# Two attention layers and two expert layers: the dispatch fill in parts, four row buffers, and a last expert that leaves by tiles

## The reference, cut to what matters

```python
x = x + L0_xattn(layernorm(x), ctx)      # quantised self- and cross-attention, softmax, projection
x = x + L0_ffn(layernorm(x))             # 8 experts, top 2, capacity 640, relu
x = x + L1_xattn(layernorm(x), positions, tokens)   # grouped attention, rms norm, rope
x = x + L1_ffn(layernorm(x))             # 8 experts, top 2, no capacity, silu(gate) * up
```

```python
h = relu(dispatched @ w1); out[token] += gate * (h @ w2)              # L0_ffn
y = (silu(x @ w_gate) * (x @ w_up)) @ w2; out[token] += gate * y      # L1_ffn
```

## Time and profile before

| | us |
|---|---|
| median of 3 runs | 3048.16 |
| lowest, highest | 3046.93, 3048.58 |
| profiled execution, its time | 3051.39 |
| its span, first to last instruction | 3049.6 |
| first attention, experts | 0 to about 1140, about 1140 to 2020 |
| second attention, experts | 2021 to 2757, 2760 to 3049.6 |

### The profile page before, as it was taken

How to read it: one execution, slowest core, us unless ns; L and a number is a source line. 1 busy time by engine, 2 the same in 40 slices (tenths; PEclk the granted TensorE clock), 3 DMA queues, 4 the chain that set the end, 5 groups by cost and what they waited for, 6 DMA issues and landing times. The chain is left out here.

```text
span 3049.6 us, 57678 instructions
## 1 busy us (share of the span) xinstructions
PE 2834.9 (93%) x16353; PEld 1636.1 (54%) x16354; DVE 1807.4 (59%) x5590; ACT 1703.4 (56%) x4562; POOL 1749.1 (57%) x2443
## 2 busy tenths in 40 slices
PE   4699999999999969999999999959999999985998
PEld 2366666666666644555555555424555555543664
DVE  4366666666666646433443444539989988863443
ACT  5578777787777742332332333427777777751332
POOL 6467777777777624544453544447677777731222
PEclk9899999999999989999999999979999999998999
DMA  7711121111211145544554454735665555557444
GB/s 244 257 43 50 56 80 59 49 49 56 80 59 49 46 142 166 158 136 138 161 154 135 139 159 136 215 76 114 122 137 132 118 131 129 127 108 292 83 81 68
DMA packets 467530, 360.90 MB, mean 118 GB/s; under 512 B 295521, under 2 KB 366305, under 8 KB 467425
## 3 DMA queue, kind: packets, MB, share of 16 engines
q1 hardware_dynamic: 404912, 282.85, 32.5%
q0 software_dynamic: 16496, 37.79, 6.2%
q10 hardware_dynamic: 46016, 38.99, 4.4%
HBM read 186.23 MB, written 110.39 MB: 97 GB/s over the span
## 5 line engine op out<-in xcount | busy, mean ns | idle before, releaser
L1393 POOL TENSOR_TENSOR e_st<-e_st,e_ws_tile 128x1024 f32<-128x1024 f32 x64 | 123.9, 1936 | 429.0 <-PE e_y L1149 417.3
L752 ACT ACTIVATE a_nrm<-a_mm,a_sc_t 128x128 f32<-128x128 f32 x768 | 290.9, 475 | 123.5 <-POOL a_sc_t L905 123.3
L603 DVE BATCH_NORM_STATS2 a_st<-a_mm 128x6 f32<-128x128 f32 x768 | 170.5, 284 | 290.5 <-PE a_mm L440 208.0
L439 PE MATMUL a_mm<-a_w_hi,a_xq_hi 128*128 128x512 f16 x768 | 296.9, 387 | 23.3 <-POOL a_xq_lo L887 15.1
L1187 ACT ACTIVATE e_hh<-e_ha 128x512 f16<-128x512 f32 x128 | 76.3, 596 | 413.3 <-PE e_ha L1134 412.0
L440 PE MATMUL a_mm<-a_w_hi,a_xq_lo 128*128 128x512 f16 x768 | 297.0, 387 | 0.0
L1282 DVE SCALAR_TENSOR_TENSOR e_hl<-e_ha,e_hh 128x512 f16<-128x512 f32 x128 | 88.4, 691 | 351.7 <-ACT e_hh L1187 351.3
L904 POOL TENSOR_TENSOR a_sc_t<-a_sc_t,a_mhalf 128x4 f32<-128x4 f32 x192 | 204.1, 1063 | 118.5 <-DVE a_sc_t L610 118.2
L1148 PE MATMUL e_y<-e_w2l,e_hh 128*128 128x512 f16 x640 | 242.6, 379 | 0.0
L1147 PE MATMUL e_y<-e_w2h,e_hh 128*128 128x512 f16 x640 | 242.6, 379 | 0.0
L1149 PE MATMUL e_y<-e_w2h,e_hl 128*128 128x512 f16 x640 | 242.6, 379 | 0.0
(11 more groups left out here) (366 smaller groups left out, 8221.4 us busy)
## 6 DMA issues: line engine op xcount, KB each, us to landing
e_st<-in_w SPq DMA_DIRECT2D x128, 512.0 KB, 4.1
disp<-a_empty SPq DMA_DIRECT2D x16, 2084.0 KB, 8.0
e_st<-in_w1b SPq DMA_DIRECT2D x32, 352.0 KB, 3.1
disp<-a_empty SPq DMA_DIRECT2D x4, 2605.0 KB, 21.5
e_xb<-disp SPq DMA_DIRECT2D x40, 260.5 KB, 4.3
e_xb<-disp ACTq DMA_DIRECT2D x40, 260.5 KB, 2.7
a_cx<-in_ctxT SPq DMA_DIRECT2D x32, 256.0 KB, 3.3
a_stage<-in_wprojT SPq DMA_DIRECT2D x16, 512.0 KB, 4.9
```

Source lines behind the costliest of these rows:

```text
L439: pe.matmul(out, xq_hi[:, n, c, :], w_hi[:, t, c, :], start=(c == 0), stop=False)
L752: ins = act.activation(nrm[:, n % 2, i * P:(i + 1) * P], src[:, i * P:(i + 1) * P], ACT.Identity, bias=sc_t[:, n % 2, 3, i:i + 1], scale=s ...
```

## The change

1. The fill of `disp` leaves SP in eight DMAs of 5 tiles, in the even slots of batch 1, after the other steps of the slot; `r_scatter` waits for eight.
2. In the last expert of the first experts PE signals each tile of Y; DVE takes tiles 0, 2, 4 and ACT 1, 3, each signals by itself, and POOL adds each tile when it is out. The row numbers are copied without a wait.
3. The second experts have four buffers for rows; four loads go ahead of the loop, then tile i+3 in `x_high(i)`. The loop body holds four tiles on PE, ACT and DVE. One more tile of rows is loaded at the end (41 for 40).
4. In `add_rows` of the second experts the row numbers are copied before the wait for the add before.

```diff
-                    for n in range(4):
-                        sp.dma_start(disp[n * TILES // 4 * P:(n + 1) * TILES // 4 * P, :].rearrange("(c p) d -> p c d", p=P),
-                                     empty[:].unsqueeze(1).to_broadcast([P, TILES // 4, RW])).then_inc(sem["disp_filled"], 16)
+            def fill_disp(b, t):
+                if isinstance(b, int) and b == 1 and t % 2 == 0:
+                    lo, hi = (n * TILES // (NJ // 2) for n in (t // 2, t // 2 + 1))
+                    sp.dma_start(disp[lo * P:hi * P, :].rearrange("(c p) d -> p c d", p=P),
+                                 empty[:].unsqueeze(1).to_broadcast([P, hi - lo, RW])).then_inc(sem["disp_filled"], 16)
...
+            run_pipeline(sp, [("job", 0, lambda b, t: weights(b, t + 1)), ("att", 5, residual), ("end", 10, store), ("in", 1, x_load),
+                              ("job", 0, fill_disp)], NJ, SCORE_AT, head=HEAD)
...
-                pool.wait_ge(sem["disp_filled"], 16 * 4)
+                pool.wait_ge(sem["disp_filled"], 16 * (NJ // 2))
...
+                    if last and c == FC - 1:
+                        mm.then_inc(y_each, 1)
+                if not (last and c == FC - 1):
+                    mm.then_inc(y_done, 1)
...
+                for i in range(1, TPE, 2) if last else range(3, TPE):
+                    if last:
+                        act.wait_ge(y_each, i + 1)
                     ins = act.activation(yb[:, i, :], Y[i][:], ACT.Copy, scale=g_now[:, i:i + 1])
+                    if last:
+                        ins.then_inc(y_out[i % 2], 1)
...
+                for i in range(0, TPE, 2) if last else range(3):
+                    if last:
+                        dve.wait_ge(y_each, i + 1)
                     ins = dve.tensor_scalar(yb[:, i, :], Y[i][:], g_now[:, i:i + 1], None, ALU.mult)
+                    if last:
+                        ins.then_inc(y_out[i % 2], 1)
...
+            def add_rows(e, last=False):
+                if not last:
+                    pool.wait_ge(ya_ok, e + 2)
+                    pool.wait_ge(yv_ok, e + 2)
                 ch.link(pool.tensor_copy(r_now[:], row[:, bass.ds(e * TPE, TPE)]))
                 for i in range(TPE):
+                    if last:
+                        pool.wait_ge(y_out[i % 2], i // 2 + 1)
...
-        xb = s.sb("xb", [P, 2, RW], F32)
+        xb = s.sb("xb", [P, XBUF, RW], F32)
...
-            whole = (most_tiles - most) // 2
+            whole = (most_tiles - most) // XBUF
             with eng.Fori(0, whole) as n:
-                for q in range(2):
+                for q in range(XBUF):
                     for ahead, f in stages:
-                        f(2 * n + q + ahead, (q + ahead) % 2)
+                        do(f, XBUF * n + q + ahead, (q + ahead) % XBUF)
...
-                if not (isinstance(i, int) and i == 0):
+                if not (isinstance(i, int) and (i == 0 or i + XBUF - 1 > last_load)):
                     act.wait_ge(meta, i + 2)
-                    load(i + 1, 1 - q)
+                    load(i + XBUF - 1, (q + XBUF - 1) % XBUF)
...
-            load(0, 0)
-            load(1, 1)
+            last_load = XBUF * ((most_tiles - 2) // XBUF) + XBUF
+            for i in range(XBUF):
+                load(i, i)
...
             def add_rows(i, q):
                 pool.wait_ge(r_ok, i + 1)
                 pool.wait_ge(yev, i + 3)
+                ch.link(pool.tensor_copy(r_now[:, q:q + 1], row[:, bass.ds(i, 1)]))
                 if not (isinstance(i, int) and i == 0):
                     pool.wait_ge(added, 16 * i)
-                ch.link(pool.tensor_copy(r_now[:, q:q + 1], row[:, bass.ds(i, 1)]))
                 pool.sem_inc(y_free, 1)
```

More of the change, by code:

```diff
@@ L956 @@
 KEYS = 2 * P
+XBUF = 4
 W_NAMES = ["K", "Q0", "Q1", "Q2", "Q3", "V"]
@@ L1135, in hidden, with second @@
                     mm.then_inc(done, 1)
-            def second(e, c):
+            def second(e, c, last):
                 m = c // 2
@@ L1156, in body @@
                         hidden(e, c + 1, last)
-                    second(e, c)
+                    second(e, c, last)
                     if c in TILE_AT and not last:
@@ L1244, in body @@
                     columns(e + 1)
-                act.wait_ge(y_done, e * FC + FC + 2)
+                if not last:
+                    act.wait_ge(y_done, e * FC + FC + 2)
                 act.wait_ge(y_free, e + 1)
                 act.wait_ge(g_ok, e + 1)
-                for i in range(3, TPE):
+                for i in range(1, TPE, 2) if last else range(3, TPE):
+                    if last:
+                        act.wait_ge(y_each, i + 1)
                     ins = act.activation(yb[:, i, :], Y[i][:], ACT.Copy, scale=g_now[:, i:i + 1])
-                ins.then_inc(ya_ok, 1)
+                    if last:
+                        ins.then_inc(y_out[i % 2], 1)
+                if not last:
+                    ins.then_inc(ya_ok, 1)
             for j in range(TPE):
@@ L1365, in body @@
                     columns(e + 1)
-                dve.wait_ge(y_done, e * FC + FC + 2)
+                if not last:
+                    dve.wait_ge(y_done, e * FC + FC + 2)
                 dve.wait_ge(y_free, e + 1)
-                for i in range(3):
+                for i in range(0, TPE, 2) if last else range(3):
+                    if last:
+                        dve.wait_ge(y_each, i + 1)
                     ins = dve.tensor_scalar(yb[:, i, :], Y[i][:], g_now[:, i:i + 1], None, ALU.mult)
-                ins.then_inc(yv_ok, 1)
+                    if last:
+                        ins.then_inc(y_out[i % 2], 1)
+                if not last:
+                    ins.then_inc(yv_ok, 1)
                 ch.clear()
@@ L2062, in layer1_experts, with pipeline, do @@
         w_in = [s.sem(f"w_in{e}") for e in range(E)]
-        x_in = [s.sem(f"x_in{n}") for n in range(2)]
+        x_in = [s.sem(f"x_in{n}") for n in range(XBUF)]
         block = s.block()
-        def pipeline(eng, stages):
+        def pipeline(eng, stages, by_buffer=()):
             most = max(n for n, _ in stages)
+            def do(f, i, q):
+                f(i, q) if f in by_buffer else f(i, q % 2)
             for i in range(-most, 0):
@@ L2071, in pipeline @@
                     if i + ahead >= 0:
-                        f(i + ahead, (i + ahead) % 2)
-            whole = (most_tiles - most) // 2
+                        do(f, i + ahead, (i + ahead) % XBUF)
+            whole = (most_tiles - most) // XBUF
             with eng.Fori(0, whole) as n:
-                for q in range(2):
+                for q in range(XBUF):
                     for ahead, f in stages:
-                        f(2 * n + q + ahead, (q + ahead) % 2)
-            for i in range(2 * whole, most_tiles):
+                        do(f, XBUF * n + q + ahead, (q + ahead) % XBUF)
+            for i in range(XBUF * whole, most_tiles):
                 for ahead, f in stages:
                     if i + ahead < most_tiles:
-                        f(i + ahead, (i + ahead) % 2)
+                        do(f, i + ahead, (i + ahead) % XBUF)
         def first_two(i):
@@ L2182, in y_evict @@
                 act.activation(yb[:, q, :], YB[q][:], ACT.Copy, scale=1.0 / (WS * WS)).then_inc(yev, 1)
-            load(0, 0)
-            load(1, 1)
-            pipeline(act, [(2, x_high), (0, a_high), (1, silu_gate), (0, y_evict)])
-            act.wait_ge(x_in[most_tiles % 2], 16 * (most_tiles // 2 + 1))
+            last_load = XBUF * ((most_tiles - 2) // XBUF) + XBUF
+            for i in range(XBUF):
+                load(i, i)
+            pipeline(act, [(2, x_high), (0, a_high), (1, silu_gate), (0, y_evict)], (x_high,))
+            for n in range(XBUF):
+                act.wait_ge(x_in[n], 16 * ((last_load - n) // XBUF + 1))
         @block.vector
```

28 lines of the change are left out of this document (12 added, 16 removed).

## The result

The changed kernel takes 3019.7 us (median; 3017.5 to 3020.9), the one before 3047.55 in the same measurement: a ratio of 0.9903, 95% interval 0.9889 to 0.9917, so 27.9 us less. The forecast was 3011; the time lies inside the range, 9 us above its point. Ratios and their intervals in this document leave out one execution of part 2 alone that took 9036.8 us.

A forecast was written before the change was run, and what follows sets the result against it. TensorE (PE), busy 93% of the span, was taken as the bound, with waits at block starts, the joint and the end. Savings 21.5 + 4.7 + 9 + 1.8 = 37.0 off 3048.2 gave 3011 us, range 3005 to 3024.

The forecast's parts named there:

- the steady batch: First attention: distance of 63.6 us between later `cx_lo` marks on POOL, forecast to return once the stall goes.
- 85.1 us: First attention: first distance between `cx_lo` marks, 21.5 longer than the steady 63.6; the basis of part 1's -21.5.
- the joint: Between first experts and second attention: evictions by tile let POOL's adds issue earlier, taken -4.7 us.
- Counted from add 0's issue at 2787: Second experts: evictions waiting for adds to free output buffers give back 0.5 to 3 us of part 3's gain.
- 42.4 - 32.1 us: Second experts, transpose 2 to 7: 42.4 us for five tiles that take 32.1 at 6.41 each; 10.3 to gain.
- The 1.37 us of transpose 2: Second experts: transpose 2's own wait, added to the 10.3 to make part 3's 11.7 in all.
- the first term: First attention: with the fill spread, the stall for the load of `xt` goes, taken -21.5 us (-19.8 to -21.7).
- Rival A: Second experts: adds take the place of the loads, gain there 3 us or less, kernel at 3017; chance 0.15.
- Rival C: Second experts: doubled loop body makes PE stand for code at each of nine passes, kernel at 3056; chance 0.02.

The follow-up runs named there:

- part 2 alone: The kernel before with only the by-tile evictions in the last of the first experts: 3044.6 us, 0.9991 of the kernel before.
- four fills behind: The kernel before with its four large fill DMAs moved as they are behind the load of xt: 3027.0 us, 0.9933 of the kernel before.
- eight ahead: The changed kernel with all eight fill parts issued at once ahead of the load of xt: 3037.3 us, 0.9965 of the kernel before.
- parts 3 and 4 together: The kernel before with four row buffers and the row-number copy before the wait, nothing else: 3043.8 against 3046.8 us, 0.9988.

## Experiments: what held the second experts

**Four output buffers** (the changed kernel; an eviction waits for the add four tiles back rather than two).
```diff
-        yb = s.sb("yb", [P, 2, DM], F32)
+        yb = s.sb("yb", [P, 4, DM], F32)
...
-            act.sem_inc(y_free, 1)
+            act.sem_inc(y_free, 3)
```


> The changed kernel with four output buffers in place of two in the second experts: y_evict(i) waits for add i-4 instead of add i-2. Theory (the adds, 10 us each while the weights come in, are what holds the tiles once the row waits are gone): the adds stay as slow as they are, but ACT's waits for POOL (14.9 us in three) go, PE's transpose of tile 11 comes about 76 us after the block's start instead of 83.9, and the kernel gains 6 to 8 us on the changed one, 3011 to 3014. Rival (rows, weights and adds share so much that PE then waits for rows or weights instead): tile 11 stays at 82 or later, 3018 to 3020.

> The changed kernel with four output buffers once more, beside the two that build on it. It was 3014.1 us, 0.9888 of the kernel before. Expected 3013 to 3016 and a ratio of 0.988 to 0.990, from the add chain's release of the evictions; 3019 or more would mean that the first measurement was an outlier and that the buffers give nothing.


Measured: 3014.1 (0.9888 [0.9872, 0.9903]) and in a second measurement 3015.9 (0.9902 [0.9886, 0.9919]), against 3019.7 (0.9903 [0.9889, 0.9917]) for the changed kernel. Neither interval excludes no gain over it, and as a difference from the kernel before in the same measurement (-32.8, -30.0 against -27.9) the two are 5 and 2 us. The traces are clearer. In the first of them the evictions wait for PE in 38 tiles and none waits for a buffer, and PE's wait for `e_al` is down from 4.3 to 1.4 us:

```profile
ACT e_yb L2208 <- PE e_y L2175: 56.9, 38, 2.9
```
```profile
PE e_y L2173 <- DVE e_al L2264: 1.4, 1, 1.4
```

while the adds still leave 9.6 and 10.4 us apart:

```profile
2760.47 1.64 POOL L2285 DMA_INDIRECT out<-e_yb,e_r_now  x1 [0.84 <-POOL e_r_now L2281]
2770.08 1.59 POOL L2285 DMA_INDIRECT out<-e_yb,e_r_now  x1 [4.06 <-DMA out<-e_yb,e_r_now]
2780.51 1.57 POOL L2285 DMA_INDIRECT out<-e_yb,e_r_now  x1 [8.17 <-DMA out<-e_yb,e_r_now]
```

All kernels, grouped by their second experts (one profiled execution each; the two with paced weights are left out):

| kernels | tile 2 to tile 11, us | first load to end, us |
|---|---|---|
| rows two buffers: before, part 1, part 2, part 4, four fills behind | 67.1 to 68.1 | 288.2 to 290.0, mean 289.0 |
| part 3 without part 4 | 66.2 | 289.3 |
| parts 3 and 4: changed, eight ahead, parts 3 and 4 | 65.2 to 65.6 | 283.7 to 286.8, mean 285.4 |
| parts 3 and 4 and four output buffers: both measurements, and with the dummies below | 59.7 to 59.9 | 280.1 to 281.4, mean 280.5 |

So parts 3 and 4 are worth 3.6 us with two output buffers and 8.5 with four, and the 4.9 between them are what the adds took back. Four output buffers without parts 3 and 4 were not run. But in none of the five traces of the first row does an eviction wait for a buffer, so there they would have had no wait to take away.

**Weights paced** (the changed kernel; SP loads the weights of experts 3 to 7 only as tiles get done).
```diff
+                if e >= 3:
+                    sp.wait_ge(w_in[e - 1], 64)
+                    sp.sem_inc(w_ok, 1)
+                    sp.wait_ge(yd, 2 * (e - 2) + 2)
...
-                if e >= 1:
+                if 1 <= e < 3:
```


> The changed kernel with SP loading the weights of experts 3 to 7 of the last block only as tiles are done (expert e after 2(e-2) tiles), two output buffers as before. Theory (adds are slow because the weights fill the DMA engines): an add goes from about 10 us to 5 or 6, the tiles run every 6.4 us from the second on, tile 11 at about 76 to 78 us, 3012 to 3015. Rival (adds are slow by themselves at first, or because of the row loads ahead): adds still 9 to 10 us apart, 3018 to 3020.


Measured: 3021.3, 0.9913 [0.9899, 0.9927]: no gain. The early stretch is repaired (tile 2 to tile 11 in 59.6 us, add 1 is issued 6.4 us after add 0), but then ACT waits 21.6 us for buffers, 20.0 of them after the transpose of tile 11, and the later adds come 8 to 10 us apart where a paced expert's weights are loaded (POOL):

```profile
2761.26 1.64 POOL L2289 DMA_INDIRECT out<-e_yb,e_r_now  x1 [0.84 <-POOL e_r_now L2285]
2767.67 1.59 POOL L2289 DMA_INDIRECT out<-e_yb,e_r_now  x1 [0.86 <-POOL e_r_now L2285]
...
2804.93 1.57 POOL L2289 DMA_INDIRECT out<-e_yb,e_r_now  x1 [4.64 <-ACT e_yb L2212]
2814.64 1.57 POOL L2289 DMA_INDIRECT out<-e_yb,e_r_now  x1 [7.93 <-remote]
```

SP issues the weights of experts 4 to 7 at 2778.6, 2791.5, 2804.2 and 2819.1. Between adds that leave 8.1 to 10.3 us apart the core's DMA engines move 217 to 324 GB/s, between those 5.6 to 6.0 apart 88 to 164, and of the two steps of 6.4 us one has 111 and one 239. An add is slow when weights are in flight, whenever that is. This ties the 10 us to the weights' traffic and not to the start of the block. Nor are the deeper row loads the cause: in the kernel before, with two row buffers, the first adds leave 10.7, 9.1 and 9.5 apart.

**Four output buffers and paced weights.** The edits are the two above.


> The changed kernel with four output buffers and with the weights of experts 3 to 7 loaded one expert per two tiles done (as a_pace, 3021.3 us). Theory (the adds are slowed by whatever else fills the DMA engines): pacing only moves the weights' traffic to later tiles; the chain of adds is early faster and later slower, and at the end it stands where it stood in a_yb4, some 3 us behind PE: 3014, within 1.5 us of a_yb4. Rival (only the burst hurts): with slack of four buffers the chain makes up its lag, the last eviction lies 12.7 us before the end instead of 15.8: 3011.


Measured: 3014.9, 0.9893 [0.9877, 0.9910], within 1.0 us of both measurements of four buffers without pacing. In the profiled execution (3022.0, the longest of its four) the adds run one behind another to the end, mostly 6.4 us apart and the last five steps 5.5, and the last eviction lies 20.7 us before the end, 8 more than in the changed kernel: the chain did not make up its lag, rather the reverse. No gain of pacing is seen.

**Work for PE ahead of the first weights** (four output buffers, and 28 and 14 dummy matmuls behind the first two transposes).
```diff
+            def x_warm(i, q):
+                x_transpose(i, q)
+                if isinstance(i, int) and i < 2:
+                    for _ in range((28, 14)[i]):
+                        pe.matmul(YB[1][:, 0:P], ones[:], upper16[:], start=True, stop=True)
...
```


> The changed kernel with four output buffers (as a_yb4, 3014.1 us), and on top of it 28 dummy matmuls (128x128, into a bank that nothing reads yet) behind the first transposes of the second experts and 14 behind the second, so that PE works while it waits for expert 0's weights. The output is the reference's. Theory (the clock): in the changed kernel the first gate_up ran for 6.1 us at the lower level of the clock, after PE had stood; in the kernel before it did so for 3.3. With work ahead of it the lower level covers 0 to 1 us, half of the rest comes back: -2 to -3, 3011 to 3012. Rival (the weights): PE gets to its second tile early and stands for the next expert's weights or for the first row loads instead: 3014, no change. Second rival: the dummy work itself delays the second tile's transpose, by up to 14 x 0.1 us: 3015 to 3016.


Measured: 3012.2, 0.9886 [0.9870, 0.9903], the lowest median of all, but its interval overlaps both of the kernel with four output buffers alone, and that of the changed kernel too. The place that was meant shows little. The first `gate_up`, without the dummies (the second measurement of four output buffers) and with them (windows as above):

```profile
2743.90:2750.10 6.20, 6.20 (x26) 3.46 (x27) 0.46 (x6) 0.81 (x1) 0.00 (x0) 0.59 1.04 405
```
```profile
2747.90:2753.20 5.30, 5.30 (x26) 3.09 (x27) 0.00 (x0) 0.00 (x0) 0.00 (x0) 0.68 1.03 404
```

The granted clock over the 26 matmuls is 0.68 in place of 0.59 and they take 0.9 us less, but they start 0.7 later, and tile 2 is reached 18.8 us after the start against 18.9. From first load to end both take 280.1. Whether the 3.7 us between the medians are the dummies' is open; this trace doesn't show them.

## Why the prediction was right or wrong

**Part 1, right.** Forecast -21.5 (-19.8 to -21.7); measured -20.7 alone. In the traces the first experts begin at 1135.4 (mean of five with the old order) and 1115.3 (mean of eight with the load ahead): -20. The stall went, the steady batch of 63 to 64 us took its place, SP's order was the one worked out. What was a little off is the base: I subtracted the steady batch from 85.1 us, of one execution. In four other kernels with the old order the same distance is 82.9, 82.9, 83.6 and 83.7, so the execution that I read had 1.4 to 2.2 us more than usual there. That is also part of the 3.2 us by which it lay above the median: the sum was made off the median, the term off the long execution. The clock came out as forecast, 1.00 after 140; before that it was 0.84, with PE busy for 19.1 of 20 us, so the whole batch did not run at full clock. I had also forecast that the parts behind the load cost nothing, and no trace shows a cost: the next steady distance is 63.6 again.

**Part 2, right, 0.7 short.** Forecast -4.7, the joint shows -4.0. I let POOL issue 0.14 us after the eviction; it took 0.77. The issue chain of 1.87 stayed the bound, as said.

**Part 3, the mechanism right, one term mis-sized.** The row waits went, and the adds took part of the gain back, as said. The step that was mis-sized is "Counted from add 0's issue at 2787: evict 4 wants its buffer 24 us later, at 2811, and add 2 lands 26.4 later [...] so 0.5 to 3 us come back". Measured 4.9 come back, the difference that four output buffers make. Three things were wrong in it. Add 2 lands not 26.4 but 29.6 us after add 0's issue (2762.04 to 2791.67, where the eviction that it releases starts): I took 1 us off each step for the copy, and the adds stayed 9.6 to 10.9 apart. The wait begins one tile earlier than I said, at the eviction of tile 3 (4.20 us), and comes again at tile 4 (6.87) and tile 5 (3.88). And ACT had more to do than I thought: it runs its stages in a fixed order, so an eviction that waits holds the split of the next tile's activation, and PE's `down` with it. A second, smaller error is the gain itself: I counted all of 42.4 - 32.1 us as row loads, but the tile 2 to 3 distance stays 8.1 to 8.6 us with any number of buffers, some 1.9 above the steady tile, for PE's first waits on ACT and DVE. With four output buffers tiles 2 to 7 take 34.0 us, and that is the most that the loads could give: -8.4 against the execution that I read. The base was high here too: the four others with two row buffers take 40.7 to 42.3 us, so against them it is -6.7 to -8.4. The 1.37 us of transpose 2 did not come back either: it starts 18.3 us after the block's start, before 18.2. Expert 0's weights arrive 0.3 later, and the first `gate_up` has 6.0 us of matmuls at a granted clock of 0.50, before 3.3.

Here the page of the Trainium skill that I weighed was the better guide. "DMA: Bandwidth & Descriptors", "Issuing engines are not separate DMA queues", has all DMAs interleave on the same engines. The trace agrees: with the weights of SP's queue in flight (DMA engines' share 1.02 to 1.04, some 400 GB/s) an add from POOL's queue takes 8.8 to 10.1 us, where it takes 4.8 later in the same kernel. From that page I put this part at -1 to -5 and the sum at 3015 to 3019. Measured are -3.6 for parts 3 and 4 together and 3019.7, just above that range. The reason was a different one than I drew from it, though: the row waits did go, and what paid for the loads' depth was the landing of the adds beside them.

**Part 4, mis-sized.** Forecast -1.8; 0.3 us a step is saved, and alone nothing is measured. I took the whole 1.0 us from landing to issue for the copy's. With the copy moved, POOL still needs most of that from the landing to the issue: the evictions that are released in between start at 2782.10 and 2791.67, and the adds are issued 0.67 and 0.66 us later, not the 0.2 that I expected. That it pays in company is likely but not shown (parts 3 and 4 together, above).

**The sum.** Forecast 37.0, measured 27.9. The miss is in the sizes and all of it to one side; nothing cancelled. Of the 9 us, about 1 is the first term, 0.7 the joint and 7 the second experts (10.8 forecast for parts 3 and 4, 3.6 measured). Rival A, at 0.15, came closer there ("the second experts gain 3 or less", measured 3.6), and the time came out nearer to its 3017 than to 3011, 2.7 us above it; I gave the adds' chain too much slack. Rival C (four tiles in the loop's body) is out: PE's steady tile is 6.3 to 6.4 us in the changed kernel as before.

## What to carry over

When a wait is taken away with deeper buffers on the input side, work through the output side of the same loop at the new pace, with the duration that its transfers have in that very stretch and not in the quiet one, and follow the engine's own order: what else stands behind the instruction that will wait. Bulk traffic that nobody needs soon goes behind the load that somebody waits for; the order in one queue was worth 20 us here and cutting the transfer up nothing. And a term read from one execution should be held against other executions of the same stretch, where there are any, before it is taken off a median: both large terms here came from an execution that stood up to 2 us above its like.

## What the runs showed of the hardware

- An indirect add of 128 rows (0.26 MB) lands 8.8 to 10.1 us after its issue while weights stream in at 400 GB/s (adds 0 to 2 of the changed kernel). In the quiet part it lands after 4.5 to 4.9 us in some executions and after 5.1 to 5.9 in others, with the chain of adds then standing one behind another at the tiles' pace. With the wait between them, one add a tile is slower than a tile of PE while the weights come in.
- From the landing of the add before it to the next issue on POOL pass at least 0.66 us even when nothing is left to compute in between (2791.67 to 2792.33); an instruction of 0.18 us taken out of that gap saved 0.3 (5.83 to 5.52 between the last two issues).
- A DMA issued behind ten megabytes of fills in SP's queue holds SP for 3 to 8 us (3.32 and 8.23 for the same load) and its data come with the last of the fills; issued ahead of them it holds it for 0.33.
- After a stretch in which PE mostly stood, its first 6.0 us of dense matmuls in the changed kernel ran at a granted clock of 0.50, which is the 1.2 GHz level, and what followed at 1.00:

```profile
2739.00:2745.30 6.30, 1.31 (x7) 0.86 (x7) 2.33 (x11) 1.91 (x3) 0.00 (x0) 0.50 1.04 416
2745.30:2751.30 6.00, 6.00 (x22) 3.10 (x22) 0.23 (x4) 0.57 (x1) 0.00 (x0) 0.50 1.02 399
2751.30:2758.00 6.70, 5.22 (x36) 3.39 (x35) 2.62 (x12) 1.55 (x3) 0.00 (x0) 1.00 1.02 410
```
